# Top-k selection in two groups instead of three, its picks beside the attention values, and three queues in another order at the turn between the blocks

## The reference

```python
# first block, per sequence (k, v, r: projections of three mixes of x and shifted x)
eku = exp(u + kt); out = (a + eku * vt) / (b + eku)     # scan over t
x = layernorm(x + (sigmoid(r) * out) @ Wo.T)
# second block
weights = (x @ router_w)[..., 0] + router_b[0]
k = int(CAP * s)                                        # 64 of 512
topv, topi = top_k(weights, k)
thr = topv[:, -1]; sel_mask = weights > thr[:, None]
kc = k - 1; sel_idx = sort(topi[:, :kc], axis=1)        # 63 tokens, in order
x_sel, pos_sel, w_sel = x[bidx, sel_idx], position_ids[bidx, sel_idx], weights[bidx, sel_idx]
m_sel = m[bidx, sel_idx, sel_idx]                       # mask at the chosen rows and columns
q, kk = rope(rmsnorm(x_sel) @ wq), rope(rmsnorm(x_sel) @ wk)   # 16 heads of 16
x1 = x_sel + softmax(q kk^T / 4 + m_sel) v @ wo
x2 = x1 + gelu(rmsnorm(x1) @ w1) @ w2
out = zeros.at[bidx, sel_idx].set(x2 * w_sel) + x * (1 - sel_mask)
x = layernorm(x + out)
```

## Time and profile before

| | us |
|---|---|
| median of 3 runs | 798.54 (793.29 to 799.27) |
| profiled execution, its own time | 797.92 |
| its span, first to last instruction | 796.2 |
| PE busy | 735.6 (92%) |
| DVE busy | 675.0 (85%) |
| ACT busy | 515.9 (65%) |
| POOL busy | 513.5 (64%) |

### The profile page before, as it was taken

One profiled execution on the slowest core, in us unless ns is written; L12 is line 12 of the kernel. 1 busy time (PEld: TensorE's weight loads), 2 busy tenths in 40 slices (PEclk: granted clock), 3 DMA queues, 4 the chain that ended last, 5 costly groups with the idle time before them and its releaser, 6 DMA issues.

```text
span 796.2 us, 13169 instructions
## 1 busy us (share of the span) xinstructions
PE 735.6 (92%) x4402; PEld 541.6 (68%) x4402; DVE 675.0 (85%) x1382; ACT 515.9 (65%) x983; POOL 513.5 (64%) x495
## 2 busy tenths in 40 slices
PE   7899999999999999899799997788999979999993
PEld 5466666666676666666566766466877667899993
DVE  6798989989898999999999999788899657558784
ACT  2668888888888878788667675745666646621120
POOL 1687878878787887777766698444676563622222
PEclk8999999999999999999999999899999999999998
DMA  8012433242323324224222222321110030000000
GB/s 230 2 51 67 134 94 105 66 132 66 114 84 93 107 66 119 80 67 131 68 66 67 70 77 66 116 77 34 49 39 23 15 93 2 1 2 28 27 21 33
DMA packets 37337, 55.40 MB, mean 70 GB/s; under 512 B 3360, under 2 KB 26528, under 8 KB 37280
## 3 DMA queue, kind: packets, MB, share of 16 engines
q1 hardware_dynamic: 34464, 46.28, 19.5%
q0 software_dynamic: 2816, 8.39, 3.6%
HBM read 35.78 MB, written 18.87 MB: 69 GB/s over the span
## 4 chain that ended last, share of the span: by engine, by line
PE 51%; DVE 25%; POOL 10%; issue 6%; ACT 4%; DMA 2%; SPq 0%; POOLq 0%; DVEq 0%; ACTq 0%
PE ps L798 12%; PE ps L803 9%; PE ps L818 7%; PE ps L1138 5%; PE ps L1152 4%; POOL arena L573 4%; PE ps L933 3%; DVE arena L1554 3%; POOL arena L589 2%; DVE arena L1606 2%; PE ps L816 2%; DVE arena L1586 2%; PE ps L1000 2%; DVE arena L1576 1%; DVE arena L1595 1%
## 5 line engine op out<-in xcount | busy, mean ns | idle before, releaser
L803 PE MATMUL ps<-halves 128*128 128x512 f32 x558 | 236.2, 531 | 0.0
L798 PE MATMUL ps<-arena,wa 128*128 128x512 f32 x384 | 203.7, 613 | 12.1 <-DVE arena L1586 4.6
L803 PEld LDWEIGHTS ps<-halves 128*128 128x128 f32 x558 | 106.4, 191 | 98.7 <-issue 90.4
L818 PE MATMUL ps<-wa,arena 128*128 128x256 f32 x512 | 132.8, 382 | 0.0
L589 POOL TENSOR_TENSOR arena<-arena 128x1024 f32<-128x1024 f32 x32 | 76.3, 2385 | 76.5 <-issue 53.1
L573 POOL TENSOR_TENSOR arena<-arena 128x512 f32<-128x512 f32 x93 | 116.8, 1285 | 6.4 <-ACT halves L1213 6.4
L798 PEld LDWEIGHTS ps<-arena,wa 128*128 128x128 f32 x384 | 70.4, 191 | 41.8 <-POOL halves L574 13.9
L1554 DVE TENSOR_TENSOR_SCAN arena<-ewb,ps 128x511 f32<-128x511 f32 x64 | 74.5, 1205 | 23.4 <-ACT ps L1185 22.0
L818 PEld LDWEIGHTS ps<-wa,arena 128*128 128x128 f32 x512 | 88.1, 192 | 6.8
L580 POOL TENSOR_TENSOR arena<-arena 128x1024 f32<-128x1024 f32 x32 | 76.1, 2379 | 23.5 <-ACT arena L1199 23.5
L1581 DVE TENSOR_TENSOR_SCAN arena<-ewb,ps 128x511 f32<-128x511 f32 x64 | 74.1, 1198 | 0.0
(11 more groups left out here) (226 smaller groups left out, 1548.0 us busy)
## 6 DMA issues: line engine op xcount, KB each, us to landing
arena<-x_chan SPq DMA_DIRECT2D x32, 512.0 KB, 4.3
out<-arena SPq DMA_DIRECT2D x32, 512.0 KB, 3.3
arena<-x_chan SPq DMA_DIRECT2D x64, 127.8 KB, 3.4
wa<-w_attn SPq DMA_DIRECT2D x1, 1024.0 KB, 7.9
wa<-w_up SPq DMA_DIRECT2D x1, 1024.0 KB, 6.6
wa<-w_down SPq DMA_DIRECT2D x1, 1024.0 KB, 5.5
wqk<-w_qk SPq DMA_DIRECT2D x1, 512.0 KB, 5.3
wv<-w_v SPq DMA_DIRECT2D x1, 256.0 KB, 5.6
```

Source lines behind the costliest of these rows:

```text
L798: mm(bank[:, o, :], wa[:, m, 0, out_part], xm[s.par][:, m, :], start=True, stop=False)
L803: last = mm(bank[:, o, :], w[:, m, out_part], x[s.par], start=False, stop=(t == 2))
L818: last = mm(psY[:, j, :], gg[s.par][:, c, tokens], wa[:, 3, c, :], start=False, stop=(c == CC - 1))
```

## The change

The groups become two, of 20 and 12 sequences. Group 0 is searched in periods 22 to 28 of the first block, two rounds a period from period 25 on, and its first four pairs are picked in period 30. Group 1 is searched wholly in attention periods 1 to 6. There are five batches of picks instead of six. Three of them write to bank 4 beside the values product (column 272) and stand in front of that product. At the turn POOL clears the value tiles and makes the gate of sequence 30 before it begins the attention, ACT takes over the first two mask copies and writes the rows of sequences 29 to 31 later, and PE projects Q and K of pair 0 before it turns a mask. x1 gets another place in the arena. The gathers of rows and masks are spread anew. In the close two up parts move in front of the turn of pair 14, and in the last MLP group `split_u` moves in front of `shares`.

```diff
-    SEQS = ((0, 16), (16, 28), (28, 32))
-    SA = 16
+    SEQS = ((0, 20), (20, 32))
+    SA = 20
+    PICKED = 272
...
         h2T = place(CC, NP * P)
+        top[0] = after_stats
         x1 = place(NP, C)
+        assert top[0] <= MIXED
@@ POOL, periods of the first block @@
                 if isinstance(at.n, int) and at.n == B - 1:
-                    attention_begun()
+                    pool.wait_ge(mixed, B)
+                    value_tiles_cleared()
                 if at.had(1) and at.back(1).exists():
                     gate_of(at.back(1))
...
                 if isinstance(at.n, int) and at.n == B - 1:
-                    value_tiles_cleared()
+                    attention_begun()
...
-                if at.n == 29:
-                    for q in range(0, 3):
-                        gather_rows(q, 1)
-                if at.n == 30:
-                    gather_rows(3, 2)
+                if isinstance(at.n, int) and at.n == B - 2:
+                    gather_rows(0, 1)
+                    gather_rows(1, 1)
@@ POOL, attention @@
+                if q in (1, 3, 7, 9):
+                    first, past, batch = {1: (4, 7, 2), 3: (7, 10, 3), 7: (10, 13, 4), 9: (13, NP, 5)}[q]
+                    for late in range(first, past):
+                        gather_rows(late, batch)
+                if q + 3 < NP:
                     gather_mask(q + 3)
-                if q == 12:
-                    for late in range(14, NP):
-                        gather_mask(late)
@@ PE, first block @@
-                if n == 19:
+                if n == 23:
                     weights_turn(0)
-                if n == 27:
+                if n == 29:
                     slots_turn(0, 5, 0)
-                if 28 <= n <= 29:
-                    picks(3 * (n - 28), 3 * (n - 28) + 3, 4, 0)
                 if n == 30:
-                    weights_turn(1)
+                    picks(0, 4, 4, 0)
@@ PE, attention @@
             def values(at, v_before):
                 pe.wait_ge(pT_done, at.n + 1)
                 pe.wait_ge(vblk_done, v_before)
+                selection_b(at.n + 2)
...
             def project_o(at):
                 pe.wait_ge(oT_done, at.n + 1)
-                selection_b(at.n + 3)
@@ selection_b @@
                 if n == 2:
-                    picks(6, 8, 6, 256)
-                if n == 3:
-                    slots_turn(1, 6, 256)
-                    weights_turn(2)
-                if n == 4:
-                    picks(8, 11, 6, 256)
+                    picks(7, 10, 4, PICKED)
                 if n == 6:
-                    picks(11, 14, 6, 256)
-                if n == 10:
-                    slots_turn(2, 6, 256)
-                if n == 11:
-                    picks(14, NP, 6, 256)
+                    slots_turn(1, 4, PICKED)
+                if n == 7:
+                    picks(10, 13, 4, PICKED)
+                if n == 8:
+                    picks(13, NP, 4, PICKED)
@@ att_period of PE @@
+                if n == 2:
+                    pe.wait_ge(values_kept, 2)
+                    weights_turn(1)
...
+                if n == 1:
+                    picks(4, 7, 6, 0)
@@ closing of PE @@
+                up(second, (1, 2))
                 hn2_turn(pair(NP - 2), NP)
-                up(second, (1, 2, 3))
+                up(second, (3,))
@@ turn of PE @@
             hn_turn(pair(0))
-            mask_turn(pair(0))
             project_qk(pair(0))
             project_v(pair(0))
+            mask_turn(pair(0))
             hn_turn(pair(1))
             mask_pick(pair(0))
             outputs(At(0, B - 1))
+            mask_turn(pair(1))
             qk_turn(pair(0), 2)
-            mask_turn(pair(1))
@@ att_period of ACT @@
-                if n == 2:
-                    rows_of(At(0, B - 1))
...
                 if n == 1:
                     variances_of(At(0, B - 1))
-                    rows_of(At(0, B - 3))
-                    logs_of(At(0, B - 1))
-                    rows_of(At(0, B - 2))
-                    roots_of(At(0, B - 1))
                 if 3 <= n:
                     oT_copy(pair(n - 3))
                 if n + 1 < NP:
                     hnT_copy(pair(n + 1))
                     mask_keep(pair(n + 1))
+                if n == 1:
+                    rows_of(At(0, B - 3))
+                    logs_of(At(0, B - 1))
+                    roots_of(At(0, B - 1))
...
+                if n in (2, 3):
+                    rows_of(At(0, B - 4 + n))
@@ turn of ACT @@
             reciprocal_of(At(0, B - 1))
+            mask_copy(pair(0))
             hnT_copy(pair(1))
...
+            mask_copy(pair(1))
             evacuation_of(At(0, B - 1))
@@ DVE, first block (now) @@
+                if n == 22:
                     token_weights(0)
+                if n == 23:
                     weights_copied(0)
                     top_round(0, 0)
+                if n == 24:
                     token_halves(0)
                     top_round(0, 1)
+                if 25 <= n <= 27:
+                    top_round(0, 2 * (n - 24))
+                    top_round(0, 2 * (n - 24) + 1)
+                if n == 28:
+                    slots_chosen(0, 0)
                     slots_chosen(0, 1)
+                if n == 29:
                     slots_copied_of(0, 5, 0)
+                    for q in range(0, 4):
                         one_hot(q)
                 if n == 30:
+                    keep_values(0, 4, 4, 0, 1)
@@ DVE, selection_early @@
                 if n == 3:
-                    keep_values(6, 8, 6, 256, 3)
+                    top_round(1, 1)
+                if n == 4:
+                    top_round(1, 4)
+                if n == 5:
+                    top_round(1, 7)
+                if n == 6:
                     slots_chosen(1, 1)
@@ DVE, selection_late @@
+                if n == 1:
+                    keep_values(4, 7, 6, 0, 2)
+                    token_weights(1)
+                    for q in range(7, 10):
+                        one_hot(q)
+                if n == 2:
+                    keep_values(7, 10, 4, PICKED, 3)
+                    weights_copied(1)
+                    top_round(1, 0)
+                if n == 3:
+                    top_round(1, 2)
+                    top_round(1, 3)
+                    token_halves(1)
+                if n == 4:
+                    top_round(1, 5)
+                    top_round(1, 6)
+                if n == 5:
+                    slots_chosen(1, 0)
+                if n == 6:
+                    slots_copied_of(1, 4, PICKED)
+                    for q in range(10, 13):
+                        one_hot(q)
+                if n == 7:
+                    keep_values(10, 13, 4, PICKED, 4)
+                    for q in range(13, NP):
+                        one_hot(q)
+                if n == 8:
+                    keep_values(13, NP, 4, PICKED, 5)
@@ DVE, MLP @@
-                if g.back(-1).below(NG):
+                if g.back(-2).below(NG):
                     shares(g.back(-1))
                     split_u(g.back(-1))
+                elif g.back(-1).below(NG):
+                    split_u(g.back(-1))
+                    shares(g.back(-1))
```

More of the change, by code:

```diff
@@ L727, in _ @@
                     rope_end(q)
-                if q == 12:
-                    for late in range(14, NP):
-                        gather_rows(late, 6)
                 if q + 2 < NP:
@@ L835, in weights_turn @@
                 for j in range(TJ):
-                    if group == 2:
-                        last = mm(ps[32 * j:32 * j + ns, 6, 384:512], weights[:, j, s0:past], ident[:, :], start=True, stop=True)
-                    else:
-                        last = nc.tensor.transpose(ps[0:ns, 4 + group, j * P:(j + 1) * P], weights[:, j, s0:past], ident[:, :])
+                    last = nc.tensor.transpose(ps[0:ns, 4 + 2 * group, j * P:(j + 1) * P], weights[:, j, s0:past], ident[:, :])
                 last.then_inc(w_turned, 1)
@@ L925, in project_qk @@
                 if at.had(1):
+                    pe.wait_ge(rope_part, at.n)
+                if at.had(2):
                     pe.wait_ge(mall_done, at.n + 1)
-                    pe.wait_ge(rope_part, at.n)
                 if at.n >= 5:
@@ L1287, in period @@
                     rows_of(at.back(3))
-                if isinstance(at.n, int) and at.n in (19, 30):
-                    rms_of({19: 0, 30: 1}[at.n])
+                if isinstance(at.n, int) and at.n == 23:
+                    rms_of(0)
             def v_copy(at):
@@ L1373, in mask_copy @@
                 act.wait_ge(mt_turned, at.n + 1)
-                act.wait_ge(mask_picked, at.n)
+                if at.had(1):
+                    act.wait_ge(mask_picked, at.n)
                 a.activation(mrt.rearrange("p (a c) k -> p a (c k)", a=2), ps[:, 2:4, 256:512], ACT.Copy).then_inc(mt_copied, 1)
@@ L1431, in closing @@
                 act.wait_ge(pv_ready, NP)
-                gelu_of(second, range(0, 1))
```

(26 more changed lines are left out.)

122 lines of the change are left out of this document (18 added, 104 removed).

## The result

The changed kernel takes 788.36 us (median of four runs, 786.49 to 789.09), the kernel before, measured beside it, 798.90. The ratio is 0.987, with a 95% interval of 0.982 to 0.992: some 10.5 us are gained where 24 were forecast, and the time lies 2.4 us above the range. The profiled execution has a span of 787.1 us and took 788.83.

What follows compares the result with a forecast made beforehand. DVE bounds the first block's late periods, TensorE and DVE wait for each other in attention, TensorE bounds the MLP. Terms -3.4 - 5.9 - 12.0 - 2.8 = -24.1 us on 797.92 give 773.8, median 774.4; range 765 to 786.

Steps and rivals of the forecast that it cites:

- part 1: Two groups in the first block, from DVE's period 18 to its last: net -3.4 us, -1 to -6.
- parts 2 and 3: Turn into the attention and twelve sequences searched there, up to period 9: together -5.9 us, 0 to -12.
- part 4: Attention periods 9 to 13, free of selection and mask waits: -12.0 us, -10 to -12.5.
- part 5: The close, where up parts stand before TensorE's turn of normalised pair 14: -2.8 us, 0 to -3.
- period 30: DVE's first-block period with 48 picks taking 5.4 us on TensorE: costs 4.1 us above 12.7.
- the choice: Choice of slots on DVE in first-block period 28: 7.6 us, the middle of two rows.
- Part 2: Turn into attention: TensorE's 4.82 us wait for ScalarE goes; period 3 begins 43.5 us after DVE's last first-block period starts.
- the chain of late slots: DVE and TensorE work setting attention periods 4 to 9; period 9 starts 113.2 us after DVE's last first-block period begins.
- rival B: Waits in attention periods 2 to 8 hold TensorE at 1.2 GHz, 5.5 us each, 812 us; chance 0.03.
- worth 0: Last MLP group: splitting u ahead of the shares ends TensorE's 1.52 us wait but gains 0.
- Rival A: Attention gathers become the bound through late masks: 799 us with four stops, 787 with two; chance 0.09.
- D: Second group's work fits no gap, attention periods 2 to 8 stay as long: 780 us, inside the forecast's 0.82.

Runs made afterwards that it cites:

- experiment 7: Changed kernel with ScalarE's row normalisations of the last sequences back ahead of its hnT copy for pair 2 at the turn: 794.57 us.
- experiment 9: Changed kernel with broadened picks in attention and, where possible, period 30, plus sequence 31's K projection ahead of period 30's picks: 781.48 us.
- experiment 1: Changed kernel with period 6's turn of the slots and the picks of attention periods 7 and 8 behind the values product: 791.67 us.
- experiments 3 and 4: Changed kernel with 24 unread extra matmuls ahead of the values product in attention periods 10 to 12, of 32 or 128 columns: 800.45 and 796.48 us.
- experiment 6: Changed kernel with attention picks writing 80 to 128 columns instead of 16 and 32: 782.87 us.
- Experiments 5: Changed kernel with the K projection of sequence 31 ahead of the picks of period 30 on TensorE: 785.14 us.
- experiment 10: Changed kernel with GpSimd's time difference, mixes of sequence 30 and gate of sequence 28 computed for 4 of 512 columns: 781.76 us.

## Why the prediction was wrong

The sum on the profiled execution was 773.8 and it is 788.8, 15.0 us more:

| step | forecast | measured | missed by |
|---|---|---|---|
| start to S18 | 0 | -3.6 | -3.6 |
| part 1, S18 to S31 | -3.4 | +8.0 | +11.4 |
| parts 2 and 3, S31 to QK 9 | -5.9 | +1.6 | +7.5 |
| part 4, QK 9 to 14 | -12.0 | -12.1 | 0 |
| part 5, the close | -2.8 | -3.0 | -0.2 |

- **Part 1, periods 18 to 21:** right. They took 13.93, 13.92, 13.93 and 13.92 us (13.95 forecast), since TensorE sets them.
- **Part 1, period 30 is the largest miss (6.7 us).** The failed step reads "Twenty-four take 2.68 us, so 48 take 5.4". The count was right, the price was that of the full clock. They took 9.6 us behind a wait that my own chain had put there ("PE can start them only when DVE's clamp is done"), and the K projection behind them was slow as well. With the wait filled and the picks broad the period took 17.7 us, so clock and wait are 5.8 of the 6.7.
- **Part 1, the choice (2.8 us of the miss):** a mis-sized term. I took 7.6 us, midway between a contended row and a free one; it was 10.4, and 5.6 with GpSimd quiet. Nothing made the middle likely: in that period GpSimd has its gate and its mixes to do, as in every period of the first block, so the row of the first block was the nearer one. The last 2 us are in three smaller terms: the token weights of 20 sequences (3.8 us instead of 2.8, in period 22), the slots and one-hots (3.9 instead of 3.2, in period 29) and the period with the halves (0.3). The rounds came out to 0.02 us.
- **Part 2:** right. TensorE's wait for ScalarE is gone, and experiment 7 brings it back with 4.4 us and more. Period 3 begins 45.7 us after S31 instead of 43.5; with broad picks it is 43.2.
- **Parts 2 and 3:** the chain of late slots was right and the clock beneath it was not. With the clock at its full level S31 to QK 9 takes 112.5 us, with 113.65 forecast. By that execution all 7.5 us that were missed are the lower clock in periods 1 to 8; the same stretch with narrow picks took 117.7 to 121.2 us from one execution to the next, so the miss is 4 to 7.5 us and not one figure, and in experiment 9 it was 117.6 with broad picks and the fall in period 6. The failed step is the sentence against rival B, "PE still had 0.97 of its clock ..., and it will wait less". TensorE did wait less at the turn, and its clock was lower all the same: behind the picks, with waits of 0.2 to 0.5 us ahead of them, and in period 6 behind the wait of 1.82 us for the slots. What stays open is why the picks of the kernel before were followed by rows at full clock. Their place behind the values product isn't the reason by itself, since experiment 1 put them back there.
- **Rival B** named the clock, but gave the waits as its cause, and most of the falls came behind picks without a wait. It had the size wrong as well: the lower level covers a part of a period, not a whole one, and costs 1.5 us where it comes behind picks (experiments 3 and 4) and 3 in period 6 (15.3 against 12.2 us), not 5.5. It had a chance of 0.03, and its half-way cases had none.
- **Parts 4 and 5:** right, as is "worth 0" for the last group.
- **Rival A:** no wait for mask rows shows in the attention. D is refuted by experiment 6: with the clock kept, S31 to QK 9 is 7.0 us shorter than before (119.5).
- **The start:** 3.6 us that no step forecast, and the change didn't make them. They are all there when DVE begins its second period; from then to S18 both kernels take 237.3 us. The first projections of TensorE wait for their weights (3.72 us before, 2.70 now), and the granted clock over 12 to 24 us is 0.76 before and 0.89 now. Experiments 5 and 7 give TensorE the same work up to there as the changed kernel and reach S18 at 272.6 and 272.5, as before, experiment 6 at 267.0. It is a spread of executions, and here it hid a part of the miss.

On period 28 the Trainium skill (SBUF — State Buffer, Who interferes with whom) says that DVE and GpSimd exclude each other at a port pair that they share; the trace agrees: 2.75 us for L1672 beside the gate, against 0.74 us for the same instruction in experiment 10. I had weighed that rule for the one-hots of the attention and not for the choice of the first block, where it was due. On the clock the skill (TensorE: Matmul & The Clock Gate, What's actually happening) ties the level to how busy the array has been. The trace agrees behind waits of 4.82 and 6.66 us, and adds that back-to-back matmuls of 16 and 32 columns, which the profile counts as busy, were followed by the lower level too.

## What to carry to other kernels

A full busy share of TensorE doesn't mean that its clock is safe. Here 24 narrow matmuls cost their own 2.8 us and then 1.55 us of what followed, so read the granted clock behind each such batch, and price the batch at the lower level where it stands behind a wait. Broader ones cost almost nothing here (2.87 instead of 2.83 us) and kept the clock at the picks themselves. A duration measured beside a quiet GpSimd is not the price beside a busy one: take the row from the same stage, not the middle.

## What the runs showed of the hardware

- Twenty-four matmuls took 2.83 us with 32 columns and 2.87 us with 128, and only the narrow ones were followed by 1.2 GHz, in three places of three against none of three.
- Behind a wait of 1.87 us 48 narrow matmuls ran at the lower level from the thirteenth on (466.3 us), and it held to 479 us; twelve wide matmuls among them didn't end it. Without the wait the first forty ran at full clock.
- The same program shows the low stretches at different places from one execution to the next (567 or 581 us), so a single period's length is no measure of an edit that touches the clock. A sum over several periods is a better one, but it spread over 3.5 us too (117.7 to 121.2).
- DVE's scan of 20 x 512 took 1.22 us beside a quiet GpSimd and 2.19 beside a busy one, a SCALAR_TENSOR_TENSOR of the same size 0.74 and 2.75. Three mixes of GpSimd took 5.51 us beside those, and 3.78 one period earlier.
